# A masked two-layer block with a quantized linear layer: first weight on another queue, x of batch 1 by halves, session parts and late chunks in another order

## The chip, the cores and the metric

The kernel runs on one core of one Trainium2 chip. The metric is the device time of one execution in microseconds (us). Times are given as the median of several runs; one further execution is profiled. TensorE multiplies matrices, ScalarE (ACT in the profile) computes activations and scaled copies, VectorE (DVE) and GpSimd (POOL) do elementwise work, SyncE (SP) issues most of the transfers.

## What is computed

32 batches of x (128 channels x 2048 times) go through a block with weights chosen by session, then through a linear layer whose operands are rounded to fp8, and are added to x:

```python
xm = x * cmask[:, :, None]
h = gelu(einsum('bct,bch->bht', xm, W_sess[session_ids]) + b_sess[session_ids][:, :, None])
o = (einsum('bht,hs->bst', h, W2) + b2[None, :, None]) * tmask[:, None, :]
w_q = fp8_e4m3(weight * 448 / max|weight|);  o_q = fp8_e5m2(o * 57344 / max|o|)
out = x + einsum('bsk,nk->bsn', o_q, w_q) / (o_scale * w_scale) + bias
```

The hidden size is 256, the linear layer is 2048 x 2048. Both maxima go over the whole tensor, so the second part can't begin before all 64 units of the first are done.

## The kernel before

**First part.** The work is cut into 64 units of 1024 times, two for each batch (`UPB = 2`). Precision is held by splitting fp32 values into a high part (type fp32r) and a low rest. Of unit `u`, TensorE does, in this order: `hidden(u, 0)` (hidden rows 0 to 127: six products of 512 columns, with xh and the high weight, xh and the low weight, xl and the high weight; the last wants `xl`), `project0(u)` (six products with the split first half of W2), `hidden(u, 1)`, and `project1(u)`. The loop over `u` does `hidden(u+1, 0)`, `project0(u)`, `hidden(u+1, 1)`, `project1(u)`. `project1(u)` has two forms: for `u` in `SPLIT_H1` (units 1 to 26) six products with split operands (L978), which need `hl1`; else plain fp32 products (L982), which have four records.

**Who prepares what.** ScalarE makes `xh` of unit u+2 (L591), two GELU passes of h0 (`hh` L597, and in place L598), one or two of h1 (L605 only for split units, L606). VectorE makes `hl` (L729), masks the output (`mask_o`, L739), takes its maximum (L744) and one scan of the big weight per unit (`scan`, L764: `SCAN_COLS` = 1368 columns, so 24 scans). POOL makes `hl1` (`split_h1_rest`, L527), then `xl` of unit u+2 (`split_x_rest`, L514), then masks the weight of a later batch (L534), then session parts (L551), then rounds a chunk of the big weight (`round_chunk`, L521 and L523). Each engine works strictly in the order of its own program; semaphores tie them.

**Weights by session.** For batches 0 to 3 (`DIRECT = 4`) the weight is loaded by session id with a value read from `sid_i`, scaled by the channel mask and split (batch 0 by ScalarE at L641 and VectorE, batches 1 to 3 by VectorE in `split_session_weight`, L698 and L693). For the others all eight session weights are loaded once into `sess_raw`, split (ScalarE L667 in one pass, POOL L551 in four parts), stored in HBM as `split_w` in two halves (L378), and loaded from there; POOL or ScalarE masks them. SyncE runs one ordered queue of waits and issues, so each of its waits holds back all that stands behind it. ScalarE issues a few small loads at the start from its own queue.

**The big weight.** After the scans its scale is known (unit `SCANS + 2` = `QUANT`), and chunks of 768 columns (43 of them) are scaled (ScalarE L617), their exponents taken (VectorE L753, L758) and rounded (POOL), one per unit from unit `QUANT + 1` on. `EARLY_CHUNKS` = 35 are done with the units, the other 8 are `late` and come after unit 63, the last four of them on VectorE behind the evacuations of tiles 4 to 7 (`CHUNK_BEHIND`).

**Second part.** Tiles y of 16 products (3.45 us each) run over `FIRST`: for batches 0 to 3 the columns n = 0, 1, 2, then column block n = 3 of all four (tiles 12 to 15), then batch by batch. Tile 12 waits, product by product, for the last chunks (`w_rounded` 33 to 43). Before a batch's tiles its rows are quantized (VectorE L837, for batches 2, 3 and 4 ahead of the tiles in `QUANT_AT`), transposed by a DMA (L427 for 2 and 3, tile `more`), and POOL adds the bias to x (`add_bias`, L557), which the evacuation (L857) adds to the product.

**At the very start** TensorE does products on a ramp (`warm_up`, L910), two of 512 columns, then the bias products, then two of 256.

The queue of the start on SyncE is:

```python
load_x_part(0)
sp.wait_ge(sid_loaded, 16)
load_session_weight(0)
load_x_part(1)
sp.wait_ge(raw_loaded[0], 16)
sp.dma_start(w2_sb[:, :, :], w2.rearrange("(j p) s -> p j s", p=P)).then_inc(params_loaded, 16)
load_session_weight(1)
sp.wait_ge(x_first[1], 16)
load_x(1)
```

## Time and profile before

| what | value |
|---|---|
| time, median of 3 runs (lowest, highest) | 838.66 us (838.33, 839.84) |
| the profiled execution's own time | 837.83 us |
| its span, first to last instruction | 836.0 us |
| mean granted TensorE clock, as a share of full speed | 0.998 |
| busy: TensorE, VectorE, ScalarE, POOL | 821.8, 482.6, 339.9, 514.8 us |
| first part (64 units) | to about 384 us |
| second part | from about 388 us to the end |

The profile gives each engine's busy time and, for each idle stretch, what released the engine. TensorE's records overlap a little because products are pipelined, so the distance between the starts of two groups is a better price than the length of a record. An engine that isn't the bound may idle at no cost.

### The profile page before, as it was taken

What the parts mean: (1) busy time and instruction counts of PE and PEld (TensorE: products, weight loads), DVE (VectorE), ACT (ScalarE), POOL (GpSimd) and SP (SyncE); (2) the same over time, 40 slices, a digit from 0 to 9 for tenths busy, and PEclk for the clock granted to TensorE, in tenths of its full rate; (3) what the DMA queues carried; (4) which work ended last, traced back from release to release, by engine and by line L of the source; (5) the groups of instructions that cost most, each with busy time, mean ns of one, the idle gap of its engine ahead of it and who ended that gap; (6) DMA issues with size and microseconds to landing.
All of it is one profiled execution on the core that took longest, in us unless ns stands there. A gap on an engine that the chain in (4) does not pass through costs nothing.

```text
span 836.0 us, 10119 instructions
## 1 busy us (share of the span) xinstructions
PE 821.8 (98%) x3523; PEld 481.1 (58%) x3570; DVE 482.6 (58%) x503; ACT 339.9 (41%) x354; POOL 514.8 (62%) x233
## 2 busy tenths in 40 slices
PE   8899999999999999999999999999999999999998
PEld 5678888777677676765444444444444444444444
DVE  6989999888888888888552323232323323232322
ACT  7889999998898889883200000000000000000000
POOL 1998999889999999995983242424242424242322
PEclk9999999999999999999999999999999999999999
DMA  7799999878767877666974777676767686868682
GB/s 277 285 375 326 334 323 345 323 278 320 304 256 299 308 296 274 252 208 227 359 242 125 244 245 251 238 261 229 267 222 274 215 281 214 282 214 280 215 252 107
DMA packets 74864, 222.08 MB, mean 266 GB/s; under 512 B 37578, under 2 KB 39634, under 8 KB 55506
## 3 DMA queue, kind: packets, MB, share of 16 engines
q1 hardware_dynamic: 73936, 220.62, 74.9%
q10 hardware_dynamic: 898, 1.09, 0.4%
q8 instruction: 16, 0.26, 0.1%
q14 instruction: 14, 0.11, 0.0%
HBM read 144.35 MB, written 69.21 MB: 255 GB/s over the span
## 4 chain that ended last, share of the span: by engine, by line
PE 93%; DMA 2%; DVE 1%; ACT 1%; issue 1%; POOL 1%; SPq 0%; DVEq 0%
PE ps_h L1042 51%; PE ps_h L951 20%; PE ps_o L966 10%; PE ps_o L982 8%; PE ps_o L978 4%; DMA more<-more 1%; DMA x_sb<-in_x 0%; DMA wt<-in_L_cond_W_sess 0%; PE ps_h L1018 0%; POOL xl L514 0%; DVE hl L729 0%; ACT h L606 0%; ACT hh L597 0%; DVE whl L698 0%; ACT wqT L667 0%
## 5 line engine op out<-in xcount | busy, mean ns | idle before, releaser
L1042 PE MATMUL ps_h<-wqT,x_sb 128*128 128x512 bf16 x1877 | 411.3, 379 | 2.4 <-ACT x_sb L676 0.2
L1042 PEld LDWEIGHTS ps_h<-wqT,x_sb 128*128 128x128 fp8e5 x1920 | 187.4, 98 | 224.7 <-ACT x_sb L676 0.3
L514 POOL TENSOR_TENSOR xl<-x_sb,xh 128x1024 fp32r<-128x1024 f32 x62 | 149.5, 2411 | 14.4 <-ACT xh L591 14.4
L951 PE MATMUL ps_h<-xh,whl 128*128 128x512 f32 x508 | 150.4, 417 | 1.9 <-POOL whl L534 1.1
L557 POOL TENSOR_TENSOR x_sb<-x_sb,bias_sb 128x2048 f32<-128x2048 f32 (+1 forms) x15 | 66.7, 4446 | 133.1 <-DMA x_sb<-in_x 133.1
L557 POOL TENSOR_TENSOR h<-h,bias_sb 128x2048 f32<-128x2048 f32 (+1 forms) x15 | 66.6, 4442 | 123.2 <-DMA h<-in_x 123.2
L857 DVE SCALAR_TENSOR_TENSOR o_and_max<-ps_h,scales,h 128x512 f32<-128x512 f32 (+1 forms) x59 | 44.0, 746 | 137.4 <-PE ps_h L1042 137.4
L857 DVE SCALAR_TENSOR_TENSOR o_and_max<-ps_h,scales,x_sb 128x512 f32<-128x512 f32 x59 | 44.2, 750 | 134.6 <-PE ps_h L1042 134.6
L951 PEld LDWEIGHTS ps_h<-xh,whl 128*128 128x128 f32 x508 | 95.1, 188 | 39.8 <-issue 17.5
L739 DVE SCALAR_TENSOR_TENSOR o_and_max<-ps_o,b_sb,steps 128x1024 f32<-128x1024 f32 (+1 forms) x65 | 82.2, 1264 | 28.5 <-PE ps_o L982 26.9
L729 DVE TENSOR_TENSOR hl<-ps_h,hh 128x1024 fp32r<-128x1024 f32 x63 | 76.8, 1219 | 11.9 <-ACT ps_h L598 11.9
L521 POOL TENSOR_TENSOR ws<-ws,wc 128x768 f32<-128x768 f32 (+1 forms) x43 | 72.2, 1678 | 18.1 <-DVE wc L758 16.6
L597 ACT ACTIVATE hh<-ps_h,hbias 128x1024 fp32r<-128x1024 f32 x63 | 70.4, 1117 | 29.0 <-PE ps_h L951 29.0
L951 PE MATMUL ps_h<-xl,whl 128*128 128x512 f32 x254 | 79.8, 395 | 0.2 <-POOL xl L514 0.2
L744 DVE TENSOR_REDUCE o_max<-o_and_max 128x1 f32<-128x1024 f32 x64 | 77.6, 1212 | 2.2
L523 POOL TENSOR_TENSOR wqT<-ws,wc 128x768 bf16<-128x768 f32 (+1 forms) x43 | 71.8, 1669 | 3.4
L606 ACT ACTIVATE h<-ps_h,hbias 128x1024 f32<-128x1024 f32 (+1 forms) x65 | 71.3, 1097 | 0.9 <-PE ps_h L951 0.9
L982 PE MATMUL ps_o<-h,w_sb 128*128 128x512 f32 x152 | 71.6, 592 | 0.0
L527 POOL TENSOR_TENSOR hl<-h,hh 128x1024 fp32r<-128x1024 f32 x26 | 62.7, 2413 | 9.6 <-ACT h L606 9.6
L598 ACT ACTIVATE ps_h<-ps_h,hbias 128x1024 f32<-128x1024 f32 x63 | 68.2, 1082 | 0.0
L591 ACT ACTIVATE xh<-x_sb 128x1024 fp32r<-128x1024 f32 x62 | 65.8, 1061 | 1.1 <-issue 1.1
L951 PEld LDWEIGHTS ps_h<-xl,whl 128*128 128x128 f32 x254 | 47.7, 189 | 12.4 <-POOL xl L514 1.4
(100 smaller groups left out, 660.2 us busy)
## 6 DMA issues: line engine op xcount, KB each, us to landing
x_sb<-in_x SPq DMA_DIRECT2D x45, 1024.0 KB, 6.9
masked_out<-o_and_max SPq DMA_DIRECT2D x32, 1024.0 KB, 6.7
o_in<-masked_out SPq DMA_DIRECT2D x32, 1024.0 KB, 9.0
out<-o_and_max SPq DMA_DIRECT2D x27, 1024.0 KB, 5.1
wqT<-in_L_ffn_weight SPq DMA_DIRECT2D x23, 684.0 KB, 9.5
wt<-in_L_ffn_weight SPq DMA_DIRECT2D x40, 384.0 KB, 5.5
h<-in_x SPq DMA_DIRECT2D x14, 1024.0 KB, 7.2
wraw<-split_w SPq DMA_DIRECT2D x28, 256.0 KB, 6.9
```

The source lines that it names most:

```text
L514: pool.tensor_tensor(xl[:, u % 2, :], x_cols(u), xh[:, u % 2, :].bitcast(fp32), ALU.subtract)\
L521: pool.tensor_tensor(v, v, c, ALU.add).then_inc(w_added, 1)
L523: pool.tensor_tensor(wqT[:, CHUNK_AT[i]], v, c, ALU.subtract).then_inc(w_rounded, 1)
L557: pool.tensor_tensor(to[:, cols], to[:, cols], bias_sb[:, cols], ALU.add).then_inc(xb_ready, 1)
L729: dve.tensor_tensor(hl[:, u % 2, :], h0_of(u), hh[:, u % 2, :].bitcast(fp32), ALU.subtract)\
L739: dve.scalar_tensor_tensor(o_cols(u)[:, cols], ps_o[:, u % 2, cols], b2_sb[:, :], window, ALU.add, ALU.mult)\
L744: dve.tensor_reduce(o_max[:, u + k:u + k + 1], o_cols(u)[:, cols], AX.X, ALU.max, apply_absolute_value=True)\
L857: dve.scalar_tensor_tensor(y_sb[:, r, cols], bank, y_scale, xs[r][:, cols], ALU.mult, ALU.add)\
L951: mm = nc.tensor.matmul(to[:, cols], whl[:, b % DIRECT, rows], xs[:, u % 2, cols], start=(k == 0), stop=(k == 2))
L966: nc.tensor.matmul(ps_o[:, u % 2, cols], w[:, :], hs[:, u % 2, cols], start=(k == 0), stop=False)
L982: mm = nc.tensor.matmul(ps_o[:, u % 2, cols], w2_sb[:, 1, :], h1[:, u % 2, cols], start=False, stop=True)
L1042: mm = nc.tensor.matmul(bank, q[:, k // 2, :, k % 2], wq[:, n, k, cols], start=(k == 0), stop=(k == KT - 1))
```

## The change

1. **Start.** SyncE issues both halves of batch 0's x one after the other, then waits for the ids and for the first weight; the load of the first weight is issued by ScalarE, behind its four first loads, after a wait for `sid_loaded` and a register load. The second group of warming products is one instead of two.
2. **Batch 1's x** comes in two halves with a semaphore each (`x_first[2]`, `x_first[3]`), and `split_x` waits for the half it needs. The load of all session weights goes ahead of those of weights 2 and 3.
3. **Session parts.** ScalarE's high parts are cut in four and placed by `SESS_AT` (unit 0: part 0; unit 1: part 1; unit 2: parts 2 and 3). POOL's low parts wait for their own.
4. **Weights of batches 2 and 3** are scaled by ScalarE (`high_session_weight`, two passes) and subtracted by POOL (`low_session_weight`) in units 1 and 3, instead of by VectorE in units 0 and 1. POOL masks batch 4's weight in unit 5 instead of 6.
5. **`SPLIT_H1`** is units 4 to 28 (25 units) instead of 1 to 26.
6. **Scans** are 1264 columns wide, 26 of them, which moves `QUANT` from 26 to 28, `EARLY_CHUNKS` from 35 to 33 and the late chunks from 8 to 10.
7. **Second part.** `QUANT_AT` is [2, 4, 10] instead of [2, 6, 10]; POOL adds the bias of batch 2 after five late chunks instead of six, that of batch 3 after eight, and rounds the last two chunks behind it.

```diff
-    SPLIT_H1 = [u for u in range(1, 27)]
+    SESS_AT = {0: (0,), 1: (1,), 2: (2, 3)}
+    SPLIT_LATE = {1: 2, 3: 3}
+    SPLIT_H1 = [u for u in range(4, 29)]
-    SCAN_COLS = 1368
+    SCAN_COLS = 1264
-    QUANT_AT = [2, 6, 10]
+    QUANT_AT = [2, 4, 10]
...
             load_x_part(0)
+            load_x_part(1)
             sp.wait_ge(sid_loaded, 16)
-            load_session_weight(0)
-            load_x_part(1)
             sp.wait_ge(raw_loaded[0], 16)
...
             sp.wait_ge(x_first[1], 16)
-            load_x(1)
+            for u in range(UPB, 2 * UPB):
+                load_x_part(u)
+            sp.dma_start(sess_raw, w_sess.rearrange("s p k -> p s k")).then_inc(sess_loaded, 16)
             for b in range(2, DIRECT):
                 load_session_weight(b)
-            sp.dma_start(sess_raw, w_sess.rearrange("s p k -> p s k")).then_inc(sess_loaded, 16)
...
+            def low_session_weight(b):
+                pool.wait_ge(raw_masked, b - 1)
+                pool.tensor_tensor(whl[:, b, HID:2 * HID], raw_sb[b], whl[:, b, 0:HID].bitcast(fp32), ALU.subtract)\
+                    .then_inc(wl_late, 1)
...
-                if u == UPB * (DIRECT - 1):
+                if u == UPB * DIRECT - 3:
                     mask_session_weight(DIRECT)
+                if u in SPLIT_LATE:
+                    low_session_weight(SPLIT_LATE[u])
...
-            for i in late[2:6]:
+            for i in late[2:5]:
                 round_chunk(i)
             pool.wait_ge(x2_more_loaded[0], 16)
             add_bias(x2_more[0], FRONT)
-            for i in late[6:]:
+            for i in late[5:8]:
                 round_chunk(i)
             pool.wait_ge(x2_more_loaded[1], 16)
             add_bias(x2_more[1], FRONT)
+            for i in late[8:]:
+                round_chunk(i)
...
+            def high_session_weight(b):
+                act.wait_ge(raw_loaded[b], 16)
+                act.activation(whl[:, b, 0:HID], raw_sb[b], ACT.Copy, scale=cmask[:, b:b + 1])
+                act.activation(raw_sb[b], raw_sb[b], ACT.Copy, scale=cmask[:, b:b + 1]).then_inc(raw_masked, 1)
...
+            act.wait_ge(sid_loaded, 16)
+            sid = act.value_load(sid_i[0:1, 0:1], min_val=0, max_val=NSESS - 1)
+            act.dma_start(raw_sb[0], w_sess[ds(sid, 1), :, :].rearrange("a c h -> (a c) h")).then_inc(raw_loaded[0], 16)
...
-                if u == 0:
+                for k in SESS_AT.get(u, ()):
+                    part = slice(k * NSESS // SESS_PARTS, (k + 1) * NSESS // SESS_PARTS)
                     act.wait_ge(sess_loaded, 16)
-                    act.activation(sess_split_r[:, :, 0:HID], sess_raw, ACT.Copy).then_inc(sess_high, 1)
+                    act.activation(sess_split_r[:, part, 0:HID], sess_raw[:, part, :], ACT.Copy).then_inc(sess_high, 1)
+                if u in SPLIT_LATE:
+                    high_session_weight(SPLIT_LATE[u])
...
-                if u + 2 < DIRECT:
-                    split_session_weight(u + 2)
...
             hidden_bias()
-            warm_up(WARM_START, BANK // 2)
+            warm_up(1, BANK // 2)
```

## Rows read from the trace of the kernel before

**Rows 1.** The page, part 1: busy us (share of span), instructions.

```profile
PE 821.8 (98%) x3523; PEld 481.1 (58%) x3570; DVE 482.6 (58%) x503; ACT 339.9 (41%) x354; POOL 514.8 (62%) x233
```

**Rows 2.** Stretches: us, busy PE, PEld, DVE, ACT, POOL (instructions), clock, DMA share, GB/s.

```profile
7.32:21.62 14.30, 14.20 (x58) 10.30 (x56) 8.73 (x16) 12.49 (x13) 3.66 (x3) 1.00 0.93 342
21.62:23.98 2.36, 0.16 (x1) 0.00 (x0) 1.24 (x2) 2.36 (x3) 2.36 (x3) 1.00 0.22 88
23.98:33.04 9.06, 8.04 (x26) 5.52 (x27) 8.99 (x8) 6.41 (x8) 9.06 (x5) 0.81 0.60 211
33.04:56.89 23.85, 22.74 (x97) 17.78 (x97) 22.12 (x18) 20.69 (x21) 22.03 (x12) 1.00 1.02 384
56.89:156.00 99.11, 99.11 (x428) 80.58 (x429) 89.95 (x71) 88.75 (x89) 93.19 (x45) 1.00 0.95 338
172.00:378.00 206.00, 206.00 (x772) 144.79 (x771) 176.65 (x176) 180.60 (x192) 197.94 (x106) 1.00 0.73 276
```

**Rows 3.** Waits of TensorE: waiter, releaser, us in total, times, longest.

```profile
PE ps_o L978 <- POOL hl L527: 2.2, 1, 2.2
...
PE ps_h L951 <- POOL whl L534: 1.1, 1, 1.1
...
PE ps_h L951 <- DVE hl L729: 0.8, 1, 0.8
```

**Rows 4.** The chain of waits in order of time: start us, us, what.

```profile
2.95 3.78 DMA wt<-in_L_cond_W_sess
...
167.84 1.39 PE ps_o L978 x6
...
170.60 1.40 PE ps_o L966 x6
172.00 1.39 PE ps_h L951 x6
173.39 1.72 PE ps_o L982 x4
...
413.87 7.89 DMA more<-more
```

**Rows 5.** Stretches of one us, columns as in rows 2.

```profile
26.00:27.00 1.00, 0.77 (x3) 0.58 (x3) 0.96 (x2) 0.15 (x1) 1.00 (x2) 0.50 0.00 0
```

**Rows 6.** Timeline of POOL: start us, us, engine line op out<-in, count, idle before.

```profile
20.32 1.30 POOL L551 TENSOR_TENSOR wqT<-wqT 128x512 fp32r<-128x512 f32 x1 [3.44 <-ACT wqT L667]
...
23.89 2.38 POOL L514 TENSOR_TENSOR xl<-x_sb,xh 128x1024 fp32r<-128x1024 f32 x1
```

**Rows 7.** Timeline of the start, ScalarE and TensorE.

```profile
2.41 1.28 ACT L633 ACT_TABLE_LOAD   x1 [2.41 <-issue]
...
6.76 0.51 ACT L641 ACTIVATE whl<-wt,cmask 128x256 fp32r<-128x256 f32 x1 [0.85 <-DMA wt<-in_L_cond_W_sess]
...
7.32 0.77 PE L951 MATMUL ps_h<-xh,whl 128*128 128x512 f32 x2
...
13.37 1.06 ACT L591 ACTIVATE xh<-x_sb 128x1024 fp32r<-128x1024 f32 x1 [1.14 <-issue]
```

**Rows 8.** Timeline of VectorE in the first units.

```profile
18.14 0.35 DVE L698 TENSOR_SCALAR whl<-wt,cmask 128x256 fp32r<-128x256 f32 x1
...
24.34 2.07 DVE L698 TENSOR_SCALAR whl<-wt,cmask 128x256 fp32r<-128x256 f32 x1
...
44.62 1.58 DVE L764 TENSOR_REDUCE w_max<-wqT 128x1 f32<-128x1368 f32 x1 [0.74 <-DMA wqT<-in_L_ffn_weight]
```

**Rows 9.** Timeline around tiles 4 to 12: POOL, VectorE, TensorE.

```profile
402.56 2.50 POOL L523 TENSOR_TENSOR wqT<-ws,wc 128x768 bf16<-128x768 f32 x1
...
412.50 1.28 DVE L837 TENSOR_SCALAR more<-o_in,scales 128x2048 fp8e5<-128x2048 f32 x1
...
421.89 10.52 PE L1042 MATMUL ps_h<-wqT,more 128*128 128x512 bf16 x47 [1.28 <-DMA more<-more]
...
427.63 1.16 POOL L523 TENSOR_TENSOR wqT<-ws,wc 128x512 bf16<-128x512 f32 x1
```

More of the change, by code:

```diff
@@ L223, in adaln_ffn @@
         x_loaded = [sem(f"x_loaded{r}") for r in range(2)]
-        x_first = [sem(f"x_first{p}") for p in range(UPB)]
+        x_first = [sem(f"x_first{u}") for u in range(2 * UPB)]
         raw_loaded = [sem(f"raw_loaded{b}") for b in range(DIRECT)]
@@ L228, in adaln_ffn @@
         wl_direct = sem("wl_direct")
+        raw_masked = sem("raw_masked")
+        wl_late = sem("wl_late")
         whl_masked = sem("whl_masked")
@@ L541, in _ @@
                     split_x_rest(u + 2)
-                if u == UPB * (DIRECT - 1):
+                if u == UPB * DIRECT - 3:
                     mask_session_weight(DIRECT)
+                if u in SPLIT_LATE:
+                    low_session_weight(SPLIT_LATE[u])
                 if u % UPB == 1 and DIRECT < (u + 3) // 2 < POOL_MASKS:
                     mask_session_weight((u + 3) // 2)
-                for k in [k for k in range(SESS_PARTS) if min(k, SESS_PARTS - 2) == u]:
+                for k in SESS_AT.get(u, ()):
                     part = slice(k * NSESS // SESS_PARTS, (k + 1) * NSESS // SESS_PARTS)
-                    pool.wait_ge(sess_high, 1)
+                    pool.wait_ge(sess_high, k + 1)
                     pool.tensor_tensor(sess_split_r[:, part, HID:2 * HID], sess_raw[:, part, :],
@@ L587, in split_x @@
             def split_x(u):
-                act.wait_ge(x_loaded[u // UPB % 2], (u // UPB + 1) // 2 * 16)
+                if u < 2 * UPB:
+                    act.wait_ge(x_first[u], 16)
+                else:
+                    act.wait_ge(x_loaded[u // UPB % 2], u // UPB // 2 * 16)
                 act.wait_ge(h1_psum, u - 1)
@@ L664, in _ @@
                         gelu1(u + 1, cols, k)
-                if u == 0:
+                for k in SESS_AT.get(u, ()):
+                    part = slice(k * NSESS // SESS_PARTS, (k + 1) * NSESS // SESS_PARTS)
                     act.wait_ge(sess_loaded, 16)
-                    act.activation(sess_split_r[:, :, 0:HID], sess_raw, ACT.Copy).then_inc(sess_high, 1)
+                    act.activation(sess_split_r[:, part, 0:HID], sess_raw[:, part, :], ACT.Copy).then_inc(sess_high, 1)
+                if u in SPLIT_LATE:
+                    high_session_weight(SPLIT_LATE[u])
                 if u % UPB == 1 and POOL_MASKS <= (u + 3) // 2 < B:
@@ L929, in hidden @@
                     if u % UPB == 0:
-                        if b < DIRECT:
+                        if b < 2:
                             pe.wait_ge(wh_direct, b + 1)
+                        elif b < DIRECT:
+                            pe.wait_ge(wl_late, b - 1)
                         else:
@@ L945, in hidden @@
                     rows = slice(part * HID + t * P, part * HID + (t + 1) * P)
-                    if part == 1 and t == 0 and b < DIRECT and u % UPB == 0:
+                    if part == 1 and t == 0 and b < 2 and u % UPB == 0:
                         pe.wait_ge(wl_direct, b + 1)
```

6 lines of the change are left out of this document (3 added, 3 removed).

## Prediction, made before the changed kernel was run

> **What bounds the kernel.** I read the page's busy times first: TensorE is busy 98% of the span [rows 1], so time can only be won where it waits, where its clock is low, or where it is given fewer products. The table by stretches says where that is [rows 2]: from 56.89 to 156 and from 172 to 378 us TensorE is busy for the whole of each stretch, while between 7.32 and 56.89 us there are holes. TensorE's list of waits names three of them [rows 3]: 2.2 us for POOL's low half of h1, 1.1 us for POOL's masked weight of batch 4, 0.8 us for VectorE's hl. The chain of waits gives the price of full work [rows 4]: a hidden group of six products costs 1.39 us, the same for the w2l/w2h group 1.40, and the h1 projection 1.39 split (L978) against 1.72 as plain fp32 (L982). A unit is thus 1.39 + 1.40 + 1.39 + 1.39 = 5.57 us split, 5.90 plain.
>
> From those prices the early stage can be sized. Before `hidden(2, 0)` stand three hidden groups, one projection, one more hidden group and the plain projection of unit 0: 4 x 1.39 + 1.40 + 1.72 = 8.7 us. Six split units follow up to `hidden(8, 0)`: 33.4 us. Together 42.1, and the trace takes 56.89 - 7.32 = 49.6. So 7.5 us are lost: 2.36 in the hole at 21.62, 1.7 by the clock (the granted clock stood at 0.50, the 1.2 GHz level, in the stretch at 26 us [rows 5]; it fell after that hole and TensorE worked some 3.4 us at half rate), 0.8 and 1.1 by the two other named waits, the rest in short waits for xl, hl and the first x. The cause of the largest is in order on POOL: it does a session part (1.30 us), the low half of h1, and each xl (2.38 us) one after another [rows 6], and unit 1 is already in the split list.
>
> **Units 1 to 3 plain, 27 and 28 split.** Three units pay 0.33 us more (+1.0), two pay 0.33 less (-0.67) in a stretch without a hole. In return POOL drops three passes of 2.4 us in units 1 to 3 and ScalarE three activations of about 1.0. With the first gone nothing makes `project1(1)` wait for POOL, so the 2.36 us hole goes and with it the fall of the clock. POOL has room for the two late splits: two subtractions of 2.4 us are 4.8 in a 5.57 us unit, and chunk rounding now begins two units later as well.
>
> **Batch 1's x by halves, part 1 of x ahead.** ScalarE waited until 13.37 us for the whole of batch 1 [rows 7], while its unit-0 activations were over at 12.2. The first 512 KB of a 1 MB transfer should land some 1.4 us sooner (512 KB at the 384 GB/s of a loaded stage [rows 2]). I put `xh(2)` at 12.4 us. This pulls ScalarE's chain 1 us forward.
>
> **The first session weight in ScalarE's queue.** SyncE issued it at 2.95 and it took 3.78 us [rows 4]. ScalarE's queue has four small issues ahead of it, then the register load, so I put the issue at 3.35 and the landing at 7.15 to 7.2. Queued behind this wait on ScalarE are the Gelu table load (1.28 us), the two small loads of lens and b2, and the first `xh`; the table load began at 2.41 [rows 7] and would begin at about 3.7, so that `xh(0)` starts some 0.4 us later, still ahead of the weight. What binds is the weight: its scaling (0.51 us, 6.76 [rows 7]) moves to about 7.2, and TensorE's first product to about 7.8 instead of 7.32 [rows 7]: +0.45. One warming product less leaves a hole of under 1 us in front; the cost taken is nothing besides, since holes of 0.93 us (before the bias products) and 1.1 us [rows 3] did not lower the clock.
>
> The Trainium skill speaks against this part (DMA: Bandwidth & Descriptors, "Issuing engines are not separate DMA queues"): transfers from different engines share the same 16 DMA engines, and a second issuer saves only issue time. By it, nothing but a later landing is to be had from the move, and the landing could slip behind x part 1; that case is a rival below.
>
> **Session parts, late weights.** ScalarE's one pass over the session weights becomes four over a quarter each, and the scaling of weights 2 and 3 (four passes of 0.4 to 0.5) comes to it; VectorE loses its two scalings and subtractions. One of those took 2.07 us where the same form took 0.35 at 18.14 [rows 8], so VectorE gains about 4 us before `hl(3)`, and the 0.8 us wait for hl goes. POOL gains two subtractions of about 0.65 us.
>
> **Walk through the first units.** With start 7.8 and the durations above: `hidden(2, 0)` at 16.5 (xl at 15.8, ready), `hidden(3, 0)` at 22.4 (xl 20.8, hl 21.7), `hidden(4, 0)` at 28.3 (xl 27.8). Before it was 33.04: 4.7 won. Then POOL is tight: ScalarE hands over weight 3 only at about 35.5, after which POOL does four large passes and the mask without a pause, and `xl(6)` is late by 0.3. SyncE's third scan load follows the second session store, so VectorE's scan lands near 41 and `hl(6)` is late by 0.5; VectorE already waited 0.74 us for that load before [rows 8]. `hidden(8, 0)` comes at 51.8 instead of 56.89. The mask of batch 4, one unit earlier, is off the path (1.1 us saved, counted in this). **Gain by unit 8: 5.1 us**, which includes the +0.45 and the +1.0. From there to 378 us TensorE is full in both.
>
> **Shorter scans, two more late chunks.** 26 scans for 24 leave VectorE 0.1 us shorter per unit, which is idle time, cost nothing. But ten chunks instead of eight are rounded after unit 63. The batch-3 quantization moves from tile 6 to tile 4. Before, it ran at 412.50, its transpose landed 7.89 us after 413.87, and TensorE waited 1.28 us at 421.89 [rows 4, 9]. Now it can run at 405 and its transpose lands near 415, where TensorE needs it at 420.6: -1.28. Against this: tile 12 starts at 420.6 + 3 x 3.45 = 431.0 and needs the last chunk in its last sixteenth, at 434.2. POOL before had the last chunk at 428.8 [rows 9]. Two more chunks (2 x 3.3 us) make 435.4; walking evacuations and adds in the new order I get 435.1. A VectorE pass beside them can stretch it: a POOL pass took 2.50 us instead of 1.65 while a quantization ran [rows 9]. Bounds of the wait: 0 to 2.5; I take 1.5, near the walk plus half a stretch. **Net here: +0.2.**
>
> The Trainium skill (SBUF — State Buffer, "SBUF: two separate sides") calls the port pair of VectorE and POOL an exclusive lock. The 2.50 us row agrees. By the rule the batch-4 quantization, due beside the last two chunks, blocks POOL for its whole length, and the wait would be 2.2 instead of 1.5 us.
>
> **Sum.** 837.83 (the profiled execution, span 836.0) - 5.1 - 0.67 + 0.2 = 832.3. That execution lies 0.83 below the median 838.66 of the runs shown, so 833.1.
>
> **Rivals.** (a) The weight lands behind x part 1: 512 KB at 384 GB/s, 1.4 us later, and all behind it: 834.5. For it: both transfers are in flight together; against: the small weight's time was 3.78 us of which little is data. 0.12. (b) The clock falls at the start, since there is less warming: half rate for 3.4 us costs 1.7: 834.8. For it: TensorE is then idle in most of 5.0 to 7.8; against: the shorter holes above. 0.12. (c) The early hole only moves: ScalarE with session parts and weights 2 and 3 feeds POOL later than my walk, and half of the 5.1 is given back: 835.6. 0.10. (d) The change doesn't do what it says, because units 1 to 3 wait for something else that comes just as late: 837.5 to 838.7, no change. 0.06. (e) Slower: the late chunks become the bound. Twelve POOL passes of late chunks 5 to 10 at 2.50 instead of 1.65 are 10.2 us more, so the last chunk comes at 445 and TensorE waits 11 us at tile 12, with 1.7 of half rate after it: 838.66 - 5.77 - 1.28 + 12.7 = 844.3. It turns into a loss once the wait is over 5.77 + 1.28 = 7.05 us, the last chunk later than 434.2 + 7.05 = 441.3 on the clock of the trace before. For it: POOL is the busiest helper there; against: only passes beside a quantization were slow. 0.06.
>
> **How the numbers follow.** The forecast has 0.54, its own bounds 830.8 (late wait 0, early waits of 0.8 gone) to 834.2 (late wait 2.5). Taking in (a) to (c) the range is 830.8 to 836.4. About 0.2% of the time, 1.7 us, is what a measurement can tell from no change: faster (below 837.0) 0.88, same 0.06, slower 0.06.
>
> **What would show it.** Right: no wait of TensorE on L978 for POOL near 22 us; no stretch at 0.50 after 6 us; `hidden(8, 0)` near 52; 156 L982 products in place of 152 and fewer L978; no wait for the transpose at tile 9, but one of 1 to 2 us in the middle of a tile near 430. Wrong: a first product later than 8.5 us, a low clock between 7 and 12 us, POOL waits on ScalarE that reach TensorE in units 3 to 6, or a wait at tile 12 above 3 us.

## The result, and where the time went

The changed kernel took 842.83 us (median of six executions, 842.49 to 844.86) against 838.67 for the kernel before beside it: ratio 1.005, interval 1.0038 to 1.0062. It is 4.2 us slower where 5.6 us less were forecast, and lies outside the range given (830.8 to 836.4). Three executions in all, one of the kernel before, one of `b_mask6` and one of `m_beststart`, took far longer than the others (3733.57, 1217.68 and 941.9 us); no interval here counts them. The profiled execution took 842.81 us with a span of 841.0 (before: 837.83 and 836.0). Part 1 of its page, to be held against [rows 1]:

```profile
PE 827.5 (98%) x3566; PEld 482.1 (57%) x3566; DVE 478.5 (57%) x501; ACT 341.1 (41%) x360; POOL 513.7 (61%) x234
```

TensorE is as busy as before by share, but for 5.7 us longer. Its list of waits shows what came in place of [rows 3] (waiter, releaser, us in total, times, longest):

```profile
PE ps_h L1072 <- DMA more<-more: 3.4, 1, 3.4
PE ps_o L944 <- DVE onehot L744: 2.1, 1, 2.1
PE ps_o L1008 <- POOL hl L533: 2.1, 1, 2.1
```

The wait for `hl` at unit 1 is gone, as is that for `whl`. But the one in front of the bias products has grown from 0.93 to 2.1 us, there is one of 2.1 for `hl` at another place, and the wait for the transposed rows has grown from 1.28 [rows 9] to 3.4.

Three landmarks cut an execution into four stages: the start of `hidden(1, 1)`, of `hidden(8, 1)`, and the first product of tile 0. The table by stretches gives these stages of the changed kernel (columns as in rows 2):

```profile
7.39:15.69 8.30, 8.29 (x31) 6.58 (x31) 5.37 (x10) 6.25 (x8) 0.43 (x1) 0.79 0.65 202
15.69:33.33 17.64, 17.64 (x67) 12.40 (x66) 14.01 (x13) 15.79 (x20) 12.56 (x9) 1.00 0.90 326
33.33:61.26 27.93, 25.22 (x95) 18.11 (x94) 20.48 (x17) 21.76 (x23) 21.14 (x11) 0.94 0.97 379
61.26:389.91 328.65, 327.77 (x1298) 240.94 (x1296) 284.31 (x272) 285.69 (x298) 301.65 (x152) 1.00 0.79 289
389.91:451.06 61.15, 57.78 (x268) 26.08 (x269) 33.16 (x42) 9.21 (x12) 59.00 (x29) 0.97 0.81 274
```

From 15.69 to 33.33 us TensorE never waits and the clock stays whole: that is the part that worked. Left of it the clock is at 0.79 of full speed; right of it 2.7 us of TensorE are idle and the clock is at 0.94; and tiles 0 to 12 lose another 3.4 us, at 0.97.

| stage (us, profiled executions) | before | as predicted | changed |
|---|---|---|---|
| 0 to `hidden(1, 1)` | 13.09 | 13.5 | 15.69 |
| to `hidden(8, 1)` | 46.69 | 41.1 | 45.57 |
| to tile 0 | 328.90 | 328.2 | 328.65 |
| to the end | 447.32 | 447.5 | 451.09 |
| span | 836.0 | 830.4 | 841.0 |

The predicted column is the sum of the prediction: +0.45 in the first stage, -5.1 and that 0.45 back in the second, -0.67, +0.2.

**First stage.** The chain of waits, VectorE, ScalarE, and TensorE (chain: start, us, what; timeline: start, us, engine line, idle before):

```profile
1.72 5.08 DMA ids_i<-in_itok_B
```

```profile
6.21 0.18 DVE L738 CAST counts_f<-counts_i 128x32 f32<-128x32 int32 x1 [1.75 <-DMA counts_i<-in__lenS]
...
7.02 0.23 DVE L744 TENSOR_SCALAR onehot<-ids_f,chan 8x32 f32<-8x32 f32 x1
...
7.89 0.51 ACT L668 ACTIVATE whl<-wt,cmask 128x256 fp32r<-128x256 f32 x1 [1.62 <-DMA wt<-in_L_cond_W_sess]
```

The 1 KB of ids, issued at 1.72, takes 5.08 us. `onehot` is ready at 7.25 and the bias products start at 7.39; in the trace of before they started at 5.97, on the same issue time of the ids to 0.03 us. The counts landed in 4.9 us instead of 3.7. What was new beside them is x part 1, half a megabyte issued at about 1.4 us instead of 3.36. The first weight is late too: it is issued at 3.41 instead of 2.95, takes 4.5 us instead of 3.78, and is scaled at 7.89 instead of 6.76 [rows 7]. The first hidden product starts at 8.45 instead of 7.32, right behind that scaling (TensorE):

```profile
8.45 0.73 PE L981 MATMUL ps_h<-xh,whl 128*128 128x512 f32 x2
```

Behind the longer hole the clock fell (stretches of one us, columns as in rows 2):

```profile
9.00:10.00 1.00, 1.00 (x4) 0.83 (x3) 0.00 (x0) 0.46 (x1) 0.00 (x0) 0.61 0.43 127
10.00:11.00 1.00, 1.00 (x4) 0.72 (x4) 0.94 (x3) 0.15 (x1) 0.00 (x0) 0.50 0.48 156
11.00:12.00 1.00, 1.00 (x4) 0.81 (x3) 0.97 (x2) 1.00 (x2) 0.00 (x0) 0.50 0.95 221
```

0.50 is the 1.2 GHz level. `hidden(1, 1)` starts 2.6 us later than before: 1.1 of it is the later first product, 1.5 came behind it, at the low clock.

**Second stage.** The chain of waits, then POOL and TensorE:

```profile
33.32 8.18 DMA split_w<-wqT
...
42.23 10.32 DMA wraw<-split_w
```

```profile
45.69 2.41 POOL L520 TENSOR_TENSOR xl<-x_sb,xh 128x1024 fp32r<-128x1024 f32 x1
52.62 1.04 POOL L545 TENSOR_TENSOR whl<-wraw,cmask 128x512 fp32r<-128x512 f32 x1 [4.52 <-DMA wraw<-split_w]
53.62 2.36 POOL L533 TENSOR_TENSOR hl<-h,hh 128x1024 fp32r<-128x1024 f32 x1
...
56.03 0.73 PE L1008 MATMUL ps_o<-hl,w2h 128*128 128x512 f32 x2 [2.12 <-POOL hl L533]
56.60 1.57 PE L981 MATMUL ps_h<-xh,whl 128*128 128x512 f32 x4
58.37 1.22 PE L981 MATMUL ps_h<-xl,whl 128*128 128x512 f32 x2 [0.20 <-POOL xl L520]
```

POOL stands still for 4.52 us before the mask of batch 4, because the weight takes 10.32 us to land. The mask stands in front of `hl1` of unit 6 in POOL's order, so `project1` waits 2.12 us for `hl1`; after that four products take 1.57 us instead of the 1.09 of undisturbed ones. TensorE was 2.6 us ahead of before at unit 4 (33.33 against 35.91) and is 1.5 us behind at `hidden(8, 1)` (61.26 against 59.78). `hidden(8, 0)` starts at 56.60, where the prediction had 51.8.

**Last stage.** SyncE, the chain, TensorE and POOL:

```profile
408.42 10.69 SPq L433 DMA_TRANSPOSE more<-more  x1
```

```profile
402.56 2.25 DVE more L865
...
408.42 16.64 DMA more<-more
```

```profile
411.31 10.52 PE L1072 MATMUL ps_h<-wqT,more 128*128 128x512 bf16 x48
425.20 12.21 PE L1072 MATMUL ps_h<-wqT,more 128*128 128x512 bf16 x48 [3.37 <-DMA more<-more]
...
436.48 1.16 POOL L529 TENSOR_TENSOR wqT<-ws,wc 128x512 bf16<-128x512 f32 x1
```

The transposition is issued 5.45 us sooner than in [rows 4] and lands 3.3 us later: 16.64 us under way instead of 7.89. TensorE waits 3.37 us, and the 48 products behind the wait take 12.21 us instead of 10.52, at a granted clock of 0.50 from 426 to 429 us. The last late chunk ends at 437.64, late, but tile 12 was late by then too, and did not wait.

### The profile page after: what moved, and what is told of

Read it like the earlier page. It is cut to its first block, busy times and chain, and to the rows that moved or that the text cites. A ratio compares the mean times of both kernels' runs of the same rounds, so it can differ in the third digit from the quotient of the medians.

```text
span 841.0 us, 10169 instructions
## 1 busy us (share of the span) xinstructions
PE 827.5 (98%) x3566; PEld 482.1 (57%) x3566; DVE 478.5 (57%) x501; ACT 341.1 (41%) x360; POOL 513.7 (61%) x234
## 4 chain that ended last, share of the span: by engine, by line
PE 91%; DMA 5%; POOL 1%; ACT 1%; DVE 1%; issue 1%; SPq 0%; ACTq 0%; DVEq 0%
PE ps_h L1072 50%; PE ps_h L981 20%; PE ps_o L996 10%; PE ps_o L1012 8%; PE ps_o L1008 3%; DMA more<-more 2%; DMA wraw<-split_w 1%; DMA split_w<-wqT 1%; DMA ids_i<-in_itok_B 1%; PE ps_h L1048 0%; POOL wqT L563 0%; POOL xl L520 0%; POOL hl L533 0%; DVE more L865 0%; PE ps_o L1072 0%
## 5 line engine op out<-in xcount | busy, mean ns | idle before, releaser
L520 POOL TENSOR_TENSOR xl<-x_sb,xh 128x1024 fp32r<-128x1024 f32 x62 | 149.7, 2415 | 15.1 <-ACT xh L608 15.1
L769 DVE SCALAR_TENSOR_TENSOR o_and_max<-ps_o,b_sb,steps 128x1024 f32<-128x1024 f32 (+1 forms) x65 | 82.2, 1264 | 29.5 <-PE ps_o L1012 26.2
L527 POOL TENSOR_TENSOR ws<-ws,wc 128x768 f32<-128x768 f32 (+1 forms) x43 | 73.2, 1702 | 14.4 <-DVE wc L788 13.1
L1012 PE MATMUL ps_o<-h,w_sb 128*128 128x512 f32 x156 | 73.4, 592 | 0.0
L533 POOL TENSOR_TENSOR hl<-h,hh 128x1024 fp32r<-128x1024 f32 x25 | 60.3, 2410 | 9.8 <-ACT h L623 9.8
```

What stands on the lines that cost most here:

```text
L520: pool.tensor_tensor(xl[:, u % 2, :], x_cols(u), xh[:, u % 2, :].bitcast(fp32), ALU.subtract)\
L527: pool.tensor_tensor(v, v, c, ALU.add).then_inc(w_added, 1)
L769: dve.scalar_tensor_tensor(o_cols(u)[:, cols], ps_o[:, u % 2, cols], b2_sb[:, :], window, ALU.add, ALU.mult)\
L1012: mm = nc.tensor.matmul(ps_o[:, u % 2, cols], w2_sb[:, 1, :], h1[:, u % 2, cols], start=False, stop=True)
```

## The experiments

Each kernel is the changed one with one thing put back, unless said otherwise. The four stages are given for all, since a median and one profiled execution can differ by which stretches of low clock fell into it.

| kernel | median us | ratio to before | to h(1,1) | to h(8,1) | to tile 0 | to the end |
|---|---|---|---|---|---|---|
| before | 838.7 | | 13.1 | 46.7 | 328.9 | 447.3 |
| changed | 842.8 | 1.0050 | 15.7 | 45.6 | 328.7 | 451.1 |
| e_start | 839.4 | 0.9999 | 14.9 | 45.4 | 328.6 | 450.2 |
| b_mask6 | 839.0 | 1.0004 | 17.1 | 42.3 | 328.6 | 448.4 |
| c_turnfirst | 842.3 | 1.0044 | 15.5 | 45.2 | 328.6 | 451.1 |
| d_quant6 | 841.3 | 1.0033 | 15.6 | 45.0 | 328.6 | 450.6 |
| a_x1late | 840.9 | 1.0024 | 16.4 | 45.7 | 328.6 | 448.3 |
| i_chunks8 | 839.7 | 1.0009 | 15.7 | 44.8 | 329.1 | 446.6 |
| h_split (on before) | 838.4 | 0.9994 | 13.0 | 47.8 | 328.9 | 447.6 |
| f_warm2 | 842.8 | 1.0041 | 17.5 | 45.3 | 328.7 | 450.2 |
| j_early | 837.9 | 0.9981 | 15.0 | 42.3 | 328.6 | 451.0 |
| m_beststart | 836.1 | 0.9962 | 17.1 | 42.2 | 329.1 | 445.8 |
| g_best | 833.5 | 0.9937 | 15.1 | 42.2 | 329.1 | 445.9 |

The kernel before had medians of 838.45 (e_start, b_mask6, c_turnfirst, d_quant6), 839.42 (a_x1late, h_split, i_chunks8, g_best) and 839.34 us (the other three) beside them, so differences between medians of different groups are good to about a microsecond, and across groups the ratios are the better measure. The intervals are given with each.

### e_start: the start queues put back

```diff
             load_x_part(0)
-            load_x_part(1)
             sp.wait_ge(sid_loaded, 16)
+            load_session_weight(0)
+            load_x_part(1)
...
-            act.wait_ge(sid_loaded, 16)
-            sid = act.value_load(sid_i[0:1, 0:1], min_val=0, max_val=NSESS - 1)
-            act.dma_start(raw_sb[0], w_sess[ds(sid, 1), :, :]...)
```

> The changed kernel with only the start's queues put back: SyncE issues x part 0, the first weight, then x part 1, and ScalarE issues no weight. One warming product and all the rest as changed. Theory A (the ids for the one-hot matrix land 1.4 us later because the 512 KB of x part 1 are ahead of them on the shared engines; the longer hole then costs the clock): the bias products start at 6.0 us instead of 7.39, no stretch at 0.50 before 14 us, hidden(1, 1) at 13.1 instead of 15.69, and the whole 2.6 us are kept to the end, since the second store of the session weights hangs on the same chain: 840.2 us. Rival B (the missing warming product is what lowers the clock): bias products at 6.0, but the clock still falls for 3.4 us, gain 1.1 to 1.4: 841.5. Rival C (the start is paid for elsewhere, because batch 4's weight lands at 52.5 whatever the start does): 842.8, no change.

Measured: 839.42 us (836.82 to 840.9), ratio 0.9999 [0.9985, 1.0013], so 3.4 us less than the changed kernel. The bias products start at 5.96 as in the trace of before, with a wait of 0.70 instead of 2.1. The wait for `hl1` (2.28 us) and that at tile 9 (2.51 us) stay. The cost of the start is thus in the queues, and it is far more than the 0.45 us for which I had entered it. But `hidden(1, 1)` starts at 14.9 us and not at the 13.1 that I expected: from the bias products to about 10.6 us TensorE works at half pace here too (two hidden products take 1.22 us, later 0.62). The profiled execution was the slowest of the ten (840.9 us); its stages give 0.8, 0.2 and 0.9 us of the gain, the last of them at tile 9.

### a_x1late: only x part 1 behind the wait for the ids

```diff
             load_x_part(0)
-            load_x_part(1)
             sp.wait_ge(sid_loaded, 16)
+            load_x_part(1)
```

> The changed kernel with one line moved: SyncE issues x part 1 behind its wait for the session ids instead of straight behind x part 0. ScalarE still issues the first weight, one warming product. Theory A (x part 1 ahead of the small id loads is what holds back the one-hot matrix): the bias products start at 6.0 to 6.4 us instead of 7.39; the first product comes with the weight, at 7.9 to 8.4. Rival B (the first weight in ScalarE's queue or the rest of that queue is what delays the ids): bias products stay at 7.1 us or later. The time: 841 to 842.5 by A, since the weight still lands behind x part 1, 842.8 by B.

Measured: 840.92 us (839.13 to 843.45), ratio 1.0024 [1.0012, 1.0036]; 1.9 us less than the changed kernel. The bias products start at 6.65 and wait for something else now:

```profile
PE ps_o L944 <- DMA bs_sb<-in_L_cond_b_sess: 1.4, 1, 1.4
```

`onehot` is early again when the 512 KB are out of its way: the delay was x part 1. But `bs_sb`, another small load of the same queue, is then last, and in this execution TensorE worked at half pace up to about 13.6 us. The first hidden product still waits for the weight and comes at 8.36 us (8.45 in the changed kernel), and behind it, at half pace, `hidden(1, 1)` comes only at 16.4. As far as the profiled execution shows, the shorter time of this kernel doesn't come from its start: the last stage is 2.8 us shorter (tile 9 waits 1.67 us, with full rate behind it) and the first 0.7 longer. So the run shows what x part 1 does to the small loads, and that these alone are not the price of the start; the weight's landing counts as well.

### f_warm2: the second warming product of 256 columns back

```diff
-            warm_up(1, BANK // 2)
+            warm_up(WARM_START, BANK // 2)
```

> The changed kernel with the second warming product of 256 columns put back, all else as changed. My theory (the start is late because the small loads of ids and counts land behind x part 1, not because of the missing product): the product runs in time in which TensorE waits anyway for the first weight, so nothing changes, 842.8 within 1 us. Rival (one product fewer lets TensorE's clock fall at the start): the low clock between 9 and 13 us goes and the time is about 1.7 us less, 841.1.

Measured: 842.84 us (839.07 to 844.24), ratio 1.0041 [1.0028, 1.0055], the median of the changed kernel to 0.01 us. The missing product costs nothing that can be told. In the profiled execution the first stage was even longer (17.5 us): the four warming products took 2.08 us at half pace, and the first hidden product came at 9.93 although the weight was scaled by 8.34.

### b_mask6: the mask of batch 4 back in unit 6

```diff
-                if u == UPB * DIRECT - 3:
+                if u == UPB * (DIRECT - 1):
```

> The changed kernel with POOL's mask of batch 4's weight back in unit 6. Theory A (moved to unit 5 it stands in front of hl1(6) while the weight, loaded from the second session store, lands only at 52.55; POOL sits idle 4.5 us): hl1(6) starts at 48 to 49, TensorE's waits of 2.1 us on L1008 and of 0.2 us for xl go, the clock doesn't fall near 57 us (1.7 us), hidden(8, 0) begins near 54.3: 838.7 us. Rival B (POOL's backlog makes hl1(6) or xl(8) late anyway): a wait of over 1.5 us remains at unit 6 or 8, 841.5 to 843.

Measured: 839.04 us (median, lowest 838.09), ratio 1.0004 [0.9993, 1.0014], 3.8 us less. POOL around the mask:

```profile
50.63 2.42 POOL L533 TENSOR_TENSOR hl<-h,hh 128x1024 fp32r<-128x1024 f32 x1 [1.08 <-ACT h L623]
52.98 2.43 POOL L520 TENSOR_TENSOR xl<-x_sb,xh 128x1024 fp32r<-128x1024 f32 x1
55.35 1.06 POOL L545 TENSOR_TENSOR whl<-wraw,cmask 128x512 fp32r<-128x512 f32 x1
```

The weight took 10.5 us here too, but now POOL does `hl1` and `xl` in that time and has no idle time before the mask; TensorE waits 0.30 us for `whl` instead of 2.12 for `hl1`. From `hidden(1, 1)` to `hidden(8, 1)` the kernels with the mask in unit 5 take 44.8 to 45.7 us (seven of them), those with it in unit 6 take 42.2 to 42.3 (four of them). The mask's place costs 3.0 us (means 45.3 and 42.2). In all seven TensorE waits 1.95 to 2.40 us for `hl1` of unit 6. In four of them half rate follows; in the other three (c_turnfirst, d_quant6, i_chunks8) it doesn't, but there the wait for `xl` just behind, made late by the same mask, is 0.7 us instead of 0.3 or less.

### h_split: the kernel before with units 1 to 3 plain

```diff
-    SPLIT_H1 = [u for u in range(1, 27)]
+    SPLIT_H1 = [u for u in range(4, 27)]
```

> The kernel before with SPLIT_H1 = units 4 to 26 and nothing else, so that three units have a plain h1 projection. Theory A (nearly all of the early gain comes from this list alone): no wait on L978 for POOL near 22 us, no stretch at 0.50 near 26 us, hidden(8, 0) at 52 to 54 instead of 56.89; 834.5 to 835.5 us. Rival B (without the session parts and late weights moved off VectorE the wait for hl takes its place): a wait of over 1.5 us for hl or for the weight of batch 2 or 3, 837 to 838.

Measured: 838.44 us (837.04 to 839.59), ratio 0.9994 [0.9985, 1.0004]: no gain, as the rival had it. POOL's wait is gone, and VectorE's took its place (TensorE, VectorE):

```profile
23.96 1.15 PE L951 MATMUL ps_h<-xh,whl 128*128 128x512 f32 x4 [1.32 <-DVE hl L729]
...
32.50 2.04 PE L951 MATMUL ps_h<-xh,whl 128*128 128x512 f32 x4 [2.44 <-DVE hl L729]
```

```profile
23.73 0.98 DVE L698 TENSOR_SCALAR whl<-wt,cmask 128x256 fp32r<-128x256 f32 x1
24.74 2.55 DVE L693 SCALAR_TENSOR_TENSOR whl<-wt,cmask,whl 128x256 fp32r<-128x256 f32 x1
```

Two passes over a late weight take 3.5 us of VectorE beside POOL, and `hl` comes 1.32 and 2.44 us late. Together with the move of those passes to ScalarE and POOL and the other parts kept in g_best the second stage takes 42.2 us, against 47.8 here; which of those parts is needed was not tested one by one.

### c_turnfirst: both transpositions ahead of the loads in SyncE's queue

```diff
             for b in range(2):
                 sp.wait_ge(q_ready, b + 2 + CUTS)
...
                 turn_more(b)
+            for b in range(2):
                 sp.wait_ge(o_stored[b], 3 * 16)
                 load_o(b + 4, b)
```

> The changed kernel with one reordering in SyncE's queue of the second part: the transpose of batch 3 is issued straight behind that of batch 2, ahead of the loads of o (batch 4), x (batches 4 and block 3) and the store of batch 0. Theory A (a transpose lands only when the some 4 MB issued before it have drained, so that quantizing at tile 4 bought nothing): it lands before 418 us instead of 425.07, TensorE's wait of 3.4 us at tile 9 and the low clock behind it go. Then tile 12 comes at 432 and meets the last late chunk, which is rounded 2 to 3.5 us too late: 840 to 841.5 us. Rival B (the transpose itself is slow, 12 us or more, wherever it stands, because chunk loads from ScalarE's queue share the engines): it still lands after 420, 842 to 843.

Measured: 842.25 us (840.13 to 844.83), ratio 1.0044 [1.0025, 1.0062], no gain where 1.3 to 2.8 us were expected. The transpositions land in 4.2 to 4.6 us and tile 9 doesn't wait, but tile 12 does (TensorE, POOL, VectorE):

```profile
410.72 20.88 PE L1073 MATMUL ps_h<-wqT,more 128*128 128x512 bf16 x94
...
434.68 0.60 PE L1073 MATMUL ps_h<-wqT,x_sb 128*128 128x512 bf16 x2 [0.27 <-POOL wqT L530]
438.26 5.50 PE L1073 MATMUL ps_h<-wqT,x_sb 128*128 128x512 bf16 x17 [2.98 <-POOL wqT L530]
```

```profile
434.85 2.12 POOL L528 TENSOR_TENSOR ws<-ws,wc 128x512 f32<-128x512 f32 x1 [0.23 <-DVE wc L789]
437.06 1.15 POOL L530 TENSOR_TENSOR wqT<-ws,wc 128x512 bf16<-128x512 f32 x1
```

```profile
418.88 0.75 DVE L886 SCALAR_TENSOR_TENSOR o_and_max<-ps_h,scales,x_more 128x512 f32<-128x512 f32 x1 [5.66 <-DMA out<-o_and_max]
```

So the 16.6 us of the transposition were the loads issued ahead of it. And two waits stood one behind the other: with the first taken away, the late chunks show 3.25 us. Part of that is again a transfer. The chain of waits runs from the last chunk back to a store of `out`, issued at 408.79 behind the transpositions, which took 9.90 us; an evacuation on VectorE waited 5.66 us for it, a chunk's exponents stood behind that, and POOL waited 1.10 us for them.

### d_quant6: the batch-3 quantization back at tile 6

```diff
-    QUANT_AT = [2, 4, 10]
+    QUANT_AT = [2, 6, 10]
```

> The changed kernel with QUANT_AT back at [2, 6, 10]. Theory A (the landing is set by what is queued and by the two more chunk loads, 0.79 MB, 2 us; not by when the quantization is done): the wait at tile 9 stays 3.4 us, within 0.5: 842.8 us, within 0.8. Rival B (issuing the transpose early into a full queue is what hurts; its issue took 10.69 us on SyncE against 1.92 before): the wait goes back to 1.3 and the clock stays up, 839 to 839.5.

Measured: 841.3 us (838.72 to 843.18), ratio 1.0033 [1.0019, 1.0047], 1.5 us less. The quantization comes 7 us later than in the changed kernel and takes three times as long beside POOL (VectorE, then SyncE):

```profile
413.07 4.56 DVE L865 TENSOR_SCALAR more<-o_in,scales 128x2048 fp8e5<-128x2048 f32 x1
```

```profile
417.72 1.23 SPq L433 DMA_TRANSPOSE more<-more  x1
```

Its transposition is issued 9.3 us later (417.72 against 408.42), takes 6.3 us, lands at 424.0, and TensorE goes on at 424.16, a microsecond sooner than in the changed kernel:

```profile
424.16 12.21 PE L1072 MATMUL ps_h<-wqT,more 128*128 128x512 bf16 x47 [2.98 <-DVE o_and_max L885]
```

The profile puts this wait down to an evacuation on VectorE that ended at 424.07, so two things were late by the same time, the rows and VectorE, which had been held up by the long quantization. With ten late chunks quantizing earlier bought nothing, since the earlier transposition only stood longer behind the loads. Both expectations missed: 842.8 within 0.8, and 839 to 839.5.

### i_chunks8: eight late chunks, 24 scans of 1368 columns

```diff
-    SPLIT_H1 = [u for u in range(4, 29)]
+    SPLIT_H1 = [u for u in range(4, 27)]
-    SCAN_COLS = 1264
+    SCAN_COLS = 1368
```

> The changed kernel with the scans back at 1368 columns, so that 8 late chunks are left and not 10, and with units 27 and 28 plain as the split list then must end at unit 26. QUANT_AT stays [2, 4, 10]. Theory A (the transpose of batch 3 lands behind what is queued, and the two more chunk loads of 0.79 MB add 2 us): it lands near 33.1 us after the first product of tile 0 as before, and the wait at tile 9 is 1.0 to 1.6 instead of 3.4 us. The two plain units cost 0.67. With the shorter wait and no low clock behind it 840 us, with the low clock 841.5. Rival B (moving the quantization is what costs): the wait stays at 3 us or more, 843.5.

Measured: 839.66 us (837.96 to 840.52), ratio 1.0009 [0.9999, 1.0019], 3.2 us less. The last stage is 4.5 us shorter, the third 0.4 longer for two split units fewer. With two loads of 384 KB fewer around it the transposition takes 13.3 us, and tile 9 waits 0.62 us with no fall of the clock behind it. That is less than in the two kernels with eight late chunks and the quantization at tile 6 (before 1.28, h_split 1.52): with eight chunks the earlier quantization is worth something, 0.7 to 0.9 us.

### j_early: start queues and mask both put back

The edits of e_start and b_mask6 together.

> The changed kernel with the start queues of before (first weight on SyncE) and the mask of batch 4 back in unit 6; late part as changed. My theory (start and mask are two separate losses of 3.4 and 3.8 us): both gains add, 842.8 - 3.4 - 3.8 = 835.6, with no wait on L1008 near 56 us, and the wait of 1.5 to 3.4 us for the transposition at tile 9 left. Rival (the two are one loss, because time won at the start is lost again at the mask or the other way round): 838.5 to 839.4, like each alone.

Measured: 837.88 us (835.16 to 838.74), ratio 0.9981 [0.997, 0.9991]. That is 4.96 us less than the changed kernel and 2.3 us more than both gains added. The first two stages did add: `hidden(8, 1)` starts at 57.28 (61.26 changed, 60.27 e_start). The rest is at tile 9:

```profile
421.15 12.19 PE L1069 MATMUL ps_h<-wqT,more 128*128 128x512 bf16 x47 [3.34 <-DMA more<-more]
```

It waits as long as in the changed kernel, and half rate follows. The twelve executions fall apart by their mean granted clock: seven at 0.996, with a median of 838.3, and five at 0.998 or 1.0, 835.2 to 837.3 with a median of 836.1. The sum I expected, 835.6, is near those five. It may be that tile 9 doesn't pull the clock down in them; only one execution, of the slower kind, was profiled, so that is not shown.

### g_best: what worked, kept, and the rest put back or mended

Start queues and two warming products as before, mask in unit 6, 24 scans and eight late chunks with `SPLIT_H1` 4 to 26, both transpositions first. Kept of the change: batch 1's x by halves, the order and placing of the session parts, weights 2 and 3 on ScalarE and POOL, units 1 to 3 plain, quantization at tile 4.

> The changed kernel with what the runs so far blame put back: the start's queues and two warming products, POOL's mask of batch 4 in unit 6, scans of 1368 columns and the split list 4 to 26 with 8 late chunks; and both transposes issued ahead of the loads in SyncE's queue. Of the change there remain x of batch 1 by halves, the session parts and late weights moved, and the plain units 1 to 3. Theory A (these parts are a gain of 3.5 to 5 us, and the transpose ahead of the loads 1.3): first product at 7.3, hidden(8, 0) at 52 to 53.5, no wait at tile 9, none at tile 12; 832.5 to 834 us. Rival B (the early gain can't be kept, since batch 4's weight waits for the second session store anyway): a wait of 2 us or more near unit 8, 835 to 837.

Measured: 833.47 us (832.64 to 835.26), ratio 0.9937 [0.9921, 0.9953], 5.3 us less than the kernel before by the ratio (5.95 between the medians) and 9.4 less than the changed one. `hidden(8, 0)` starts at 54.41, a little later than the 52 to 53.5 that I expected. TensorE's waits, start to end:

```profile
PE ps_o L942 <- DVE onehot L742: 1.0, 1, 1.0
PE ps_h L979 <- POOL whl L547: 0.7, 1, 0.7
...
PE ps_h L979 <- DVE hl L757: 0.2, 1, 0.2
```

### m_beststart: g_best with the changed start queues

```diff
             load_x_part(0)
-            sp.wait_ge(sid_loaded, 16)
-            load_session_weight(0)
             load_x_part(1)
+            sp.wait_ge(sid_loaded, 16)
...
+            act.wait_ge(sid_loaded, 16)
+            sid = act.value_load(sid_i[0:1, 0:1], min_val=0, max_val=NSESS - 1)
+            act.dma_start(raw_sb[0], w_sess[ds(sid, 1), :, :]...)
```

> The mended kernel (833.5: old start queues, two warming products, mask in unit 6, 24 scans, eight late chunks, both transpositions first) with the changed start queues put into it: both parts of x first on SyncE, first weight on ScalarE. My theory: the bias products come 1.4 us later and TensorE is at half rate behind them, as in the changed kernel: 3.4 us more, 836.9. Rival (the start costs only the 0.45 us of the later first weight, the rest was chance of the clock): 833.9.

Measured: 836.07 us (lowest 835.08), ratio 0.9962 [0.9949, 0.9975]: 2.6 us more than g_best, in a kernel where nothing later hides or doubles it. The bias products start at 7.22, the wait before them is 2.0 us, and all the stages behind the first are the same to 0.1 us. The first stage is 2.0 us longer and the span 1.9. This is the price of the changed start with two warming products: less than my theory (3.4), and more than four times what the prediction had. Two other pairs of kernels differ in the start's queues alone, with one warming product: by the ratios to the kernel before they give 4.3 us (changed, e_start) and 1.9 (b_mask6, j_early), this pair 2.1, each good to about 1.5.

## Why the prediction was wrong, point by point

**What bounds the kernel: right.** From `hidden(8, 1)` to tile 0 TensorE is all but full in every variant: 328.6 us with split units up to 28, and with those up to 26 it is 329.1 in the kernels made from the changed one and 328.9 in before and h_split. Every gain and loss was in the stretches the prediction had named as having holes, and in the last one, where it had seen one hole of 1.28 us.

**The start: the step that failed is its list of what the moves touch.** I priced the first weight only, and took the transfer queued behind it (x part 1, in front) as free. The sum should have held every small load that TensorE's first products need: the ids and counts were issued at the same times as before, yet with 512 KB more under way the counts landed 1.2 us later and the ids were read 1.4 us later. The weight itself was mis-sized as well: issued at 3.41, as forecast (3.35), it took 4.5 us and not the 3.78 carried over, so that the first hidden product came at 8.45 and not at 7.8. How much of that is x part 1's doing is open: with the old queues it took 3.8 us in two kernels (before, h_split) and 4.2 to 4.3 in three (e_start, j_early, g_best). The Trainium skill (DMA: Bandwidth & Descriptors, "Issuing engines are not separate DMA queues") says that loads of different engines share the same 16 DMA engines; the trace agrees, and the rule was cited in the prediction but applied to the weight alone. Rival (a) had the cause, x part 1 in front, and the amount, 1.4 us, but that is what it cost the ids; the weight, where (a) had put it, lost 0.7 at most. Rival (b), the fall of the clock, came with it, not instead of it. The argument against (b), that holes of 0.93 and 1.1 us had not lowered the clock, was of no use once the hole became 2.1 us; nor does it hold for short holes, since e_start, j_early and g_best lost the clock there behind holes of 0.70, 0.89 and 1.02 us. In place of +0.45 stand 2.6 us in the profiled execution, and 1.9 to 4.3 between kernels that differ in the start alone (2.1 for m_beststart against g_best). The missing warming product, which (b) blamed, is not the cause: with it the time is the same (f_warm2), and g_best has it and loses the clock.

**Units 1 to 3 plain, late weights off VectorE: the mechanism was right.** No wait for `hl1` in unit 1, no low clock after it, and 17.64 us without a gap to unit 4. From `hidden(1, 1)` to `hidden(4, 0)` it took 14.5 us instead of 19.95, 5.5 less where the walk had 5.2. Where nothing disturbs it (b_mask6, j_early, g_best, m_beststart) the second stage takes 42.2 us; the prediction had 41.1, the trace of before 46.69. So 4.5 of 5.5 us came there, and h_split shows that the plain units give nothing of it alone.

**The mask of batch 4, "one unit earlier, is off the path": the second step that failed.** The prediction gives the load of that weight no time at all. The load is issued at 42.23 into a stretch that moves 379 GB/s on average and took 10.32 us. The row to price it by was in the trace of before, where the two loads of this form issued between 43 and 46 us took 9.4 and 10.7. The page's median over all 28, 6.9 us, would have misled: by it the weight lands at 49.1, just after POOL's `xl` of 45.69. And the prediction did not ask what is queued behind the wait on POOL. It is `hl1(6)`. Price: 3.0 us, 2.1 of it the wait in the changed kernel, the rest half rate and `xl`. With the load taking ten microseconds the mask's place in unit 6 was the right one.

**Units 27 and 28 split: mechanism right, size a little less.** 156 records of L1012 instead of 152, as predicted. The third stage is 0.25 us shorter than before (328.65 against 328.90), and 0.4 to 0.5 shorter than in i_chunks8 and g_best, which are nearer to the changed kernel in all else, instead of 0.67.

**The late part: the third step that failed.** "Now it can run at 405 and its transpose lands near 415" had the quantization right (406.04) and the landing wrong by ten microseconds. I carried the duration of 7.89 us from [rows 4] to another place in the queue. Before, the transposition was issued 7.3 us after the last of the loads ahead of it (406.54 to 413.87); after, 0.6 us behind it (407.80 to 408.42), when 3.8 MB of `o_in`, `out` and two loads of x had been issued in the last 2.2 us. The last of those loads, in SyncE's timeline of the kernel before and of the changed one:

```profile
406.54 0.50 SPq L362 DMA_DIRECT2D x_sb<-in_x  x1
```

```profile
407.80 0.50 SPq L368 DMA_DIRECT2D x_sb<-in_x  x1
```

The transposition lands when these have been drained: 14.9 to 16.6 us behind them in the six kernels with ten late chunks and the quantization at tile 4, 13.3 with two chunk loads fewer, 4.2 to 4.6 with nothing ahead. So the place in the queue made the earlier quantization all but useless, and the two more late chunks, which the prediction had charged to POOL alone, made the landing later than before: each brings a load into the same stretch. Counted from the first product of tile 0 the rows landed after 33.4 to 35.2 us in those six kernels, after 33.1 before and after 32.4 in i_chunks8. The term -1.28 became +2.1 plus 1.7 of half rate. The other term of the sum, +1.5 for the last chunk, was hidden in the changed kernel by this wait and appeared in c_turnfirst with 3.25 us, against 0 to 2.5 as bounds: the walk gave 435.1 for the last chunk, and it came at 438.2, in part because VectorE waited for the store of `out`, which no term of the walk held.

**The rule on the ports of VectorE and POOL.** The Trainium skill (SBUF — State Buffer, "SBUF: two separate sides") calls the shared port pair an exclusive lock. The traces agree in both directions: a quantization of 1.28 us took 4.56 beside POOL (d_quant6), POOL's passes of 1.64 took 2.51 and 2.62 beside quantizations. What the prediction made of it, that the batch-4 quantization would block POOL in its last two chunks, is seen in one pass only, 2.13 us at 434.27 for 512 columns where the other of these took 1.16.

**The rivals.** Of the forecast's 0.54 nothing is left to defend: three terms failed and all in one direction. Rival (e), the slower one, had 844.3 and the place nearly right (the second part, at 425 instead of 434), but by another mechanism; POOL's passes were not slow, as (e) needed, so that its number lies near the measured 842.8 is luck. (a) and (b) were treated as exclusive, and both came. What was missing is a case in which an early load comes late.

**What was put together afterwards.** Starting from the 841.0 us of the changed kernel, g_best's stages give -0.6, -3.3, +0.5 and -5.2, together the 8.7 us between the two spans (832.3). Against the kernel before they give +2.0, -4.5, +0.2 and -1.4.

## What to carry to other kernels

A transfer has no duration of its own: it has a place in what is already under way, so take its price from a row with the same bytes ahead of it, not from a median, and when a big load is put in front, list every small load that the first products need. When a wait of an in-order helper is moved forward, look at what stands behind it; and before you enter a gain from work moved earlier, check that the queue in front of its result is not moved earlier with it.

## What the runs showed of the hardware

- **A transposition by DMA behind queued loads blocks the queue that issues it.** SyncE spent 10.69 us on the instruction that issues it (7.09 to 10.19 in the six other kernels with this order and the quantization at tile 4; 1.23 to 2.14 where the loads had been issued seven us or more earlier), so everything behind it in SyncE's order came as late as well. In c_turnfirst and g_best, with nothing ahead, each took 1.23 to 1.28 us.
- **The clock at the start differs between executions and kernels with the same hole.** With the old start queues, e_start, j_early and g_best reached `hidden(1, 1)` at 14.9 to 15.1 us, part of it at half pace, with a hole of 0.7 to 1.0 us before the bias products, while the kernel before and h_split, with 0.9 and 0.6, did so at 13.0 and 13.1. The first weight was scaled at 7.2 to 7.3 us in those three and at 6.8 in these two, though it was issued at the same time (2.95 to 2.97). With the changed queues it was 15.5 to 17.5. Executions of one kernel spread by up to 5 us (839.1 to 844.2 for f_warm2). In the trace of f_warm2 the granted clock reads as full in every microsecond from 5 to 17, while from 11.15 to 13.71 us a product starts every 0.43 us, against every 0.23 us from 14.75 on, so at the very start the spacing of the products is the thing to read. What decides between the cases stays open.
- **The fall of the clock adds to a long wait, and its length alone doesn't tell whether.** Of waits at tile 9 those of 0.62, 1.28, 1.52, 1.67 and 2.37 us were followed by full-rate products (10.52 us for a tile group), those of 2.51 (twice), 2.98, 3.34 and 3.37 by half rate for a part (12.2 us). At unit 6, though, waits of 2.12, 2.17, 2.28 and 2.40 us were followed by half rate and those of 1.95, 2.04 and 2.21 were not.
